# One chunk's convolution shared with VectorE, and two ScalarE steps of the first chunk moved, in the state space stage of a four-layer kernel

## What is computed

```python
def _L1_attn_ref(x, in_proj_w, conv_w, conv_b, x_proj_w, dt_proj_w, dt_proj_b, A_log, D, out_proj_w, norm_w):
    xn = x * jax.lax.rsqrt(jnp.mean(x * x, axis=-1, keepdims=True) + EPS) * norm_w
    xi, res = jnp.split(xn @ in_proj_w, 2, axis=-1)          # 256 channels each
    xc = conv_general_dilated(xi, conv_w, ...) + conv_b       # 4 taps along time, per channel
    xi = _silu(xc)
    delta, Bm, Cm = jnp.split(xi @ x_proj_w, [64, 80], axis=-1)
    delta = jax.nn.softplus(delta @ dt_proj_w + dt_proj_b)
    A = -jnp.exp(A_log)                                       # 256 channels x 16 states
    # state = exp(delta A) * state + delta * Bm * xi ;  y_t = sum over the 16 states of state * C_t
    _, ys = jax.lax.scan(step, state0, (deltaA, deltaB_u, Cm))
    y = (ys + xi * D) * _silu(res)
    return y @ out_proj_w + x
```

## Time and profile before

| | |
|---|---|
| time, median of 3 runs | 1232.14 us (1229.09 to 1233.37) |
| the profiled execution: its time / its span | 1222.57 us / 1220.7 us |
| busy share of the span: PE / DVE / ACT / POOL | 80% / 77% / 61% / 68% |
| front of the state space stage | 441 to 472 us of the span |
| its eight chunks of units | 472 to 977 us |

### The profile page before, as it was taken

The page is one execution under the profiler, slowest core; times in us unless marked ns, Lnnn a source line. Parts: engine busy times, 40 slices in busy tenths (PEclk is TensorE's granted clock), DMA queues, the critical chain, the costliest instruction groups (busy, mean ns, idle before and its releaser), DMA issues. The chain is left out here.

```text
span 1220.7 us, 17047 instructions
## 1 busy us (share of the span) xinstructions
PE 982.1 (80%) x4202; PEld 596.9 (49%) x4202; DVE 946.0 (77%) x2295; ACT 741.5 (61%) x1656; POOL 835.1 (68%) x604
## 2 busy tenths in 40 slices
PE   5888868289999977788989988898857736999970
PEld 3666756268888842333333433342413224777750
DVE  6999999753333337799999999999999965777760
ACT  4867747165555557967686776667833215777740
POOL 3333339647527646788999988796949967767676
PEclk9999879589999988998999889999968867999995
DMA  9996002226525425253545353534335315756543
GB/s 271 158 156 179 1 8 20 35 50 92 83 69 92 86 37 125 95 156 124 164 146 173 128 164 102 174 122 138 125 102 151 107 41 90 123 103 122 106 94 65
DMA packets 140032, 133.50 MB, mean 109 GB/s; under 512 B 14578, under 2 KB 121186, under 8 KB 139810
## 3 DMA queue, kind: packets, MB, share of 16 engines
q1 hardware_dynamic: 107106, 115.55, 35.1%
q0 software_dynamic: 32832, 16.86, 12.3%
HBM read 98.66 MB, written 31.60 MB: 107 GB/s over the span
## 5 line engine op out<-in xcount | busy, mean ns | idle before, releaser
L1900 POOL TENSOR_TENSOR ss_HC<-ss_Hs,ss_Cb 128x512 f32<-128x512 f32 x256 | 330.3, 1460 | 75.0 <-DVE ss_Hs L1952 56.3
L1625 PE MATMUL ss_Y<-ss_HC,g_ident 128*128 128x512 f32 x512 | 269.3, 657 | 49.4 <-POOL ss_HC L1900 46.2
L1952 DVE TENSOR_TENSOR_SCAN ss_Hs<-ss_dA,ss_dBu 128x512 f32<-128x512 f32 x256 | 296.8, 1199 | 8.0 <-ACT ss_dA L1801 8.0
L1801 ACT ACTIVATE ss_dA<-ss_delta,g_A 128x510 f32<-128x510 f32 x256 | 168.9, 712 | 94.2 <-DVE ss_Hs L1952 94.0
L858 POOL DMA_INDIRECT rows<-m_XS,g_slot x128 | 178.8, 1397 | 60.3 <-issue 33.6
L1625 PEld LDWEIGHTS ss_Y<-ss_HC,g_ident 128*128 128x128 f32 x512 | 97.3, 205 | 203.1 <-POOL ss_HC L1900 131.6
L1151 PE MATMUL m_x_UP<-g_m_w,m_x_gT 128*128 (+1 forms) x532 | 192.4, 468 | 0.0
L1944 DVE TENSOR_TENSOR ss_dBu<-ss_duP,ss_Bb 128x512 f32<-128x512 f32 x256 | 163.0, 683 | 1.5 <-ACT ss_duP L1781 1.5
L1171 PEld LDWEIGHTS m_x_DP<-g_m_w,m_x_hT 128*128 128x128 f32 x908 | 121.8, 191 | 62.2 <-issue 34.5
L1171 PE MATMUL m_x_DP<-g_m_w,m_x_hT 128*128 (+1 forms) x908 | 140.8, 285 | 2.3 <-ACT m_x_hT L1243 2.3
L1243 ACT ACTIVATE m_x_hT<-m_x_HP 128x256 f32<-128x256 f32 (+1 forms) x188 | 80.4, 428 | 87.2 <-PE m_x_HP L1161 85.5
(11 more groups left out here) (284 smaller groups left out, 1746.5 us busy)
## 6 DMA issues: line engine op xcount, KB each, us to landing
ss_Bb<-bc_rows SPq DMA_DIRECT2D x64, 512.0 KB, 4.6
ss_Cb<-bc_rows SPq DMA_DIRECT2D x64, 512.0 KB, 3.8
rows<-g_Z SPq DMA_DIRECT2D x2, 5031.0 KB, 53.4
m_x_G<-rows SPq DMA_DIRECT2D x156, 64.5 KB
out_rows<-m_x_YO SPq DMA_DIRECT2D x156, 64.0 KB
g_m_w<-in_w_up SPq DMA_DIRECT2D x1, 2816.0 KB, 11.3
g_m_b<-in_b SPq DMA_DIRECT2D x1, 2160.0 KB, 11.5
g_X<-in_x SPq DMA_DIRECT2D x4, 512.0 KB, 6.1
```

Of the source, the lines that this page charges most:

```text
L1625: ins = nc.tensor.matmul(Yp[:, h, :], ident[:], HC[(c * N + n) % NHC][:, h, :], start=False, stop=n == N - 1)
L1801: nc.scalar.activation(dA[n % NA][:, h, :, 1:S], seqs(delta[v][:, h, :])[:, :, 1:S], ACT.Exp, scale=A[:, h, n:n + 1]).then_inc(dA_ready.se ...
L1900: nc.gpsimd.tensor_tensor(HC[(c * N + n) % NHC][:, h, :], Hs[n % 4][:, h, :], Cb[g % 2][:, n % 2, :], ALU.mult).then_inc(hc_ready.sem, 1)
L1952: v_.tensor_tensor_scan(Hs[n % 4][:, h, :], dA[n % NA][:, h, :, :].rearrange("p s t -> p (s t)"), dBu[:, h, :], 0.0, ALU.mult, ALU.add).th ...
```

## The change

Half 1 of chunk 0 is convolved by four VectorE instructions (one product, three multiply-adds) into `yg`, which nothing else uses that early; TensorE convolves half 0 alone. `add_normalised(1)` goes from the front to unit 14 of chunk 0. In chunk 0, `powers(4)` is issued ahead of `silu_xi(1, ...)` instead of behind it ("its unit four ahead of the silu"), nothing is issued for it at n = 1, `log_dt(1)` goes from n = 2 to n = 6 and GpSimd's softplus steps from n = 3..6 to n = 7..10. `sent` goes from 12 to 14. The semaphore `sp_passed` had no reader.

```diff
-        sp_passed = m.sem("sp_passed")
+        first_conv = m.sem("first_conv")
...
-                        sp.sem_inc(sp_passed, 1)
...
-                    ins.then_inc(conv_ready.sem, 1)
+                    ins.then_inc(conv_ready.sem, 2 if c == 0 else 1)
...
-                for h in range(2):
-                    convolve(0, h, q[h])
+                convolve(0, 0, q[0])
...
-                        act.wait_ge(conv_ready.sem, conv_ready.after(c, h + 1))
+                        if c == 0 and h == 1:
+                            act.wait_ge(first_conv, K + 1)
+                        else:
+                            act.wait_ge(conv_ready.sem, conv_ready.after(c, h + 1))
...
-                        if ahead < N:
+                        if (c, n) == (0, 0):
+                            powers(ahead, c, v)
+                            powers(ahead + 1, c, v)
+                        elif (c, n) == (0, 1):
+                            pass
+                        elif ahead < N:
                             powers(ahead, c, v)
...
-                        if n == 2 and back:
+                        if n == (6 if c == 0 else 2) and back:
                             log_dt(c + 1)
...
+                        if (c, n) == (0, 14):
+                            add_normalised(1)
...
-                add_normalised(1)
-                silu_xi(0, 0, q)
+                silu_xi(0, 0, [q[0], yg[:, 1, :]])
...
-                        if back and 3 <= n < 7:
-                            softplus_step(pool, nc.gpsimd, n - 3, c + 1, 1 - v)
+                        k = n - (7 if c == 0 else 3)
+                        if back and 0 <= k < 4:
+                            softplus_step(pool, nc.gpsimd, k, c + 1, 1 - v)
...
+                dve.wait_ge(in_copied.sem, in_copied.after(0, 2))
+                acc = seqs(yg[:, 1, :])
+                v_.tensor_scalar(acc, xpad[:, 1, :, 0:S], conv_w[:, 1, 0:1], None, ALU.mult).then_inc(first_conv, 1)
+                for k in range(1, K + 1):
+                    dve.wait_ge(first_conv, k)
+                    v_.scalar_tensor_tensor(acc, xpad[:, 1, :, k:k + S], conv_w[:, 1, k:k + 1], acc, ALU.mult, ALU.add).then_inc(first_conv, 1)
...
-        sent = 3 * HT // 4
+        sent = HT - 2
```

## The result

| | before | changed |
|---|---|---|
| first series: median (range, runs) | 1229.09 us (1228.18 to 1233.37, 7) | 1236.70 us (1233.35 to 1239.21, 7) |
| ratio, 95% interval | | 1.0057, 1.0038 to 1.0076 |
| profiled execution: time / span | 1222.57 / 1220.7 us | 1233.35 / 1231.5 us |

The change made the kernel slower. I had forecast 0.9932, so the forecast was wrong in sign and by 1.3%. The kernel was timed four more times beside the experiments: 1.0001, 1.0038, 1.0030 and 1.0043. So it was slower by 0.3 to 0.6% in four series and level in one. What parts these is the subject of the last experiments, which don't settle it. (The ratios leave out one execution of the kernel before, of 3352 us, in the third series.)

A forecast was written before the change was run, and what follows sets the result against it. VectorE's work, two stalls and the front were taken to bound it: 3.4 + 5.3 + 1.5 = 10.2, less 2.5, plus 0.9, makes -8.6; with +0.3, -8.3 us: 1214.3 profiled, 1223.8 median (0.9932), range 1219 to 1228.5.

The forecast's parts named there:

- The front: Ahead of the first unit: VectorE's convolution of half 1 is ready in time, so the first unit starts 3.4 us earlier.
- Unit 4 and the logarithm: Chunk 0's dA stalls of 3.2 and 4.8 us go, a new 2.7 us stall comes in unit 5: 5.3 us less.
- The statistics: Behind unit 6 of chunk 0: fewer GpSimd instructions are in the way, about 1.5 us of unit 7's 10.2 us gain.
- What GpSimd gives back: From unit 7 to the first gate: GpSimd's list, without a gap, takes 2.5 us of the 10.2 back; gate at 544.3.
- From then on both engines repeat the pattern of before: Behind the first gate, once 0.9 us comes again: both engines work as before, gates included, so the stage keeps 8.6 us.
- The term of -8.6: The whole stage: 10.2 us gained by unit 7, 2.5 taken back by GpSimd, 0.9 regained; ends 7.7 and 10.2.
- `sent`: Behind the stage: two more stores at its end delay the next block 1.2 to 2.5 us; net -0.3 to +1.2, taken +0.3.
- Slower: Rival, chance 0.06: du of chunk 1 comes late and stalls VectorE; at 20 us late, 1235.
- TensorE's clock: Rival, chance 0.07: chunk 1's convolution at half clock, 5.2 us more into unit 5's stall; gain 3.1, 1229, no difference.

The follow-up runs named there:

- a3: The changed kernel with the logarithm back at n = 2 and the softplus steps at n = 3 to 6 in chunk 0; 0.9993 of before.
- b2: The changed kernel with the second batch's scales moved behind unit 2 of chunk 1 and `sent` at 12; 0.9941 of before.
- b3: The kernel before with the front's part alone: VectorE's convolution of half 1, and `add_normalised(1)` at n = 14; 0.9989 of before.
- b5: The changed kernel with one more GpSimd product, read by nobody, behind unit 9 of chunk 0; timed only once, no ratio given.
- d3: c4 with `sent` at 14; 0.9986 of before.
- e1: The changed kernel with a GpSimd memset of 128 x 2800 ahead of the second reweighting in the next block; 1.0103 of before.
- e2: The changed kernel, unedited, timed beside e1 on the fifth chip; 1.0043 of before.
- c4: b2 with the logarithm at n = 5 and the softplus steps at n = 6 to 9; 0.9950 of before.
- d4: The changed kernel with `sent` at 13; 1.0027 of before.
- b1: The changed kernel, unedited, on a second chip; 1.0001 of before.
- a1: The changed kernel with the second batch's scales moved from behind unit 10 of chunk 0 to behind unit 1 of chunk 1; 0.9985 of before.

## Why the prediction was wrong

In the profiled pair the forecast of -8.3 us stands against +5.3 (the 10.8 without the 5.5 ahead of the stage). Of the 13.6 us between them 6.8 lie in the stage (-1.8 for -8.6), 5.9 behind it (+6.2 for +0.3) and 1.0 in the rest.

**The front (-3.4 us): right in kind.** The first unit came 3.8 to 4.0 us earlier in a3, b2, b3, b5, d3, e1 and e2, and 2.4 to 3.5 in the others, with TensorE's convolution: in b2 its 8 passes took 3.60 us at a granted clock of 1.00, in the changed kernel's first trace 4.63 at 0.78, for the 4.05 that I had taken. Four VectorE instructions took 2.84 us for my 3.0; the gathers beside them did no harm.

**Unit 4 and the logarithm (-5.3 us): right.** One stall is left, in unit 5, 2.30 us for 2.7 forecast.

**The statistics (-1.5 us): right in kind.** They took 3.9 us for 5.2 forecast, and unit 7 came 11.1 us earlier, for 10.2. In b2, c4, d4, e2 and four others L1407 took 1.32 us instead of 0.16, and they 5.1; in d4 and e2 the first gate came 1.2 us later for it, counted from unit 6.

**The failing step is "What GpSimd gives back".** It walks GpSimd's list from unit 7 to the gate and lets VectorE run freely beside it ("where VectorE alone would reach 541.8"). But behind unit 10 VectorE has the seven scale operations of the second batch, which the text ahead of the prediction names ("finishes their scales behind unit 10") and for which my sum has no term. They cost 8.3 us more than before at unit 11; with them out of the way (b2) the last update came 2.5 us earlier than in the changed kernel. I had worked out myself that GpSimd "is never idle again in chunk 0", and had read in the earlier trace rows that a 128x8 operation took 2.40 us. That row showed a wait for GpSimd, but only for one product: it ended at 509.77, the product at 509.74, and GpSimd went straight on (509.68). From the trace of before I could have put a wait of one to two products there, not the 9.46 us over six of them; no row of it shows a wait over a run of products that long.

The Trainium skill, "SBUF — State Buffer", section "SBUF: two separate sides", has the lock that I cited and then weighed only against the gathers; it says that whoever starts first holds the ports "for the whole instruction". Here a waiting VectorE instruction didn't get its turn between GpSimd's instructions either, over up to seven of them, in b5. The row of 2.40 us and the rows of 0.99 and 2.28 shown above agree with the sentence.

**"From then on both engines repeat the pattern of before": too high.** Even without the loss the 7.4 us at b2's first gate are 4.9 at the second, 3.9 at the third and 4.3 at the last update. Chunk 1 took 60.2 us from gate to gate (57.7 before), because the seven scale operations now stand in it: 2.3 us, from 547.30 to 549.59. The wait for TensorE at its end grew by only 0.2, to 1.40. Chunk 2 gave up another 1.0, with a wait of 1.45 us for TensorE at its end (0.45 before). The 0.9 us that TensorE's clock was to give back behind the gate didn't come, though its four matmuls took 1.98 us as forecast. So the good forecast of b2's gate (103.26 for 103.0) is in part luck. VectorE was there at 100.8 without the scales, where I had it at 100.5 with them; on its way it waited 2.17 us for rows of B, a wait that my sum doesn't have. And b2's ratio, 0.9941 for 0.9932 forecast, doesn't bear the sum out either: the stage in its trace gained 4.3 us, not 8.6. The term of -8.6 should have been some -4.3 with the scales moved, and was -1.8 as the change stands.

**`sent` (+0.3 us): nearly right in two series, wrong in four.** The boundary moved 2.7 us, for 2.5 at most in my sum, and was given back where there is no gap (34.68 for 34.73 in b1); where there is, the block after came 4.7 to 7.8 us later than in the trace of before. Nothing in the trace of before points to this gap, and by the five series of the changed kernel it is what parts "no change" from "slower". Its cause stays open.

**The rivals.** "Slower" had 0.06, for du of chunk 1. That wasn't late: in the changed kernel no dBu and no scan behind unit 5 waits for du or dA. "TensorE's clock" came true at about 1 us of its size in the traces with the fast front: in b2 chunk 1's convolution took 9.88 us at a granted clock of 0.72, for 8.80 at 0.81 in the changed kernel's first trace, and unit 5 waited 3.38 us for 2.30. So unit 6 came at 51.07 and 51.23: what the front gained beyond 2.7 us was gone there. It isn't what made the kernel slower.

## What to carry to other kernels

When work moves onto GpSimd's list or later in it, look for every small VectorE operation on SBUF operands in the stretch where GpSimd will be behind, and price it with two bounds: one GpSimd instruction, and all that GpSimd has *ready*. Both were measured here for the same operation. It is cheap where GpSimd waits for VectorE's next result, here just behind a gate (0.19 and 1.19 us), and it shows as busy time, not as a wait: look for a duration that doesn't fit its size. A gain on one engine is kept only as far as the next one has idle time, and is to be followed through the next chunks as well; what is moved out of the way has to be paid where it goes. Moving work across the end of a block changes what the next block meets, so time such a part alone, and on more than one chip.

## What the runs showed that I had not expected

A VectorE operation of 0.18 us took 9.46 and 11.74 us beside GpSimd's products; scans and products with an operand in PSUM (dBu 1.27 us, scan 2.32 for two) ran at their usual times beside the same products, up to the row ahead of the reciprocal. GpSimd doesn't pay for it: its rows of 2.92 and 3.07 us overlap, and their starts lie 2.3 to 2.5 us apart as elsewhere; the run of six products beside a1's 5.73 us took 7.97 us, and 7.98 in b2 with no VectorE operation waiting. It isn't every small operation: the reciprocal ahead of it took 0.22 each time, and in b2 L1422 took 0.19 with a product running and L1423 the 1.19 until its end. TensorE's clock behind a boundary differed between executions: 32 products of L740 took 4.07 us in a1 and 6.83 in a3, at a granted clock of 0.64 and 0.50 (1.2 GHz throughout) over the 12 us around them, after the same idle time of 11.84 us.
